# A two-layer graph network on one core: deeper buffer rings and longer lags in the message stages

## The reference, cut to what matters

```
h = relu(layernorm(x));  x = x + layer0(h, edge_attr_16, edge_attr_4, src, dst)
h = relu(layernorm(x));  x = x + layer1(h, edge_attr_3, edge_attr_64, src, dst)

layer0, for each edge:  w = silu(edge_scalars @ Wfc1) @ Wfc2            (192 weights)
    e = (h @ Wl1)[src];  mid = products of w, e and edge_attr_4
    n = mean of mid over the edges with the same dst;  out = sc + alpha(n) * (n @ Wl2)
layer1, for each edge:  w = relu(edge_feature @ W_fc1) @ W_fc2          (224 weights)
    xs, xv = (h @ W_nl)[dst];  tp = products of w, xs, xv and the unit vector of edge_attr_3
    agg = sum of tp over the edges with the same src / 32;  out = gated(agg @ W_out + h @ W_skip)
```

## Time and profile before

| | |
|---|---|
| median of 3 runs | 12,249.92 us (12,239.58 to 12,279.39) |
| the profiled execution | 12,298.2 us, its span 12,296.4 us |
| messages, layer 0 | about 2,794 to 7,952 us |
| messages, layer 1 | about 8,718 to 12,010 us |
| busy shares of the span | PE 60%, DVE 61%, POOL 59%, ACT 41% |
| DMA engines | 20% for the software queue (POOL), 17.5% for SP's |

### The profile page before, as it was taken

How to read it: one execution, slowest core, us unless ns; L and a number is a source line. 1 busy time by engine, 2 the same in 40 slices (tenths; PEclk the granted TensorE clock), 3 DMA queues, 4 the chain that set the end, 5 groups by cost and what they waited for, 6 DMA issues and landing times. The chain is left out here.

```text
span 12296.4 us, 187070 instructions
## 1 busy us (share of the span) xinstructions
PE 7410.2 (60%) x31320; PEld 4866.9 (40%) x31320; DVE 7443.2 (61%) x21099; ACT 4992.3 (41%) x16585; POOL 7196.8 (59%) x7101
## 2 busy tenths in 40 slices
PE   4444444445555555555555555577667777777777
PEld 3222222222222222222222222255566666666667
DVE  6444444445565565555555565576667777777763
ACT  2333333333333333333333333343445555555553
POOL 4666666656666666666666666555555666665650
PEclk7555555557777777777777777788899999999999
DMA  2222222223333333333333334444444444444465
GB/s 80 74 74 74 73 73 72 74 69 108 106 109 107 109 110 108 108 109 107 107 108 109 109 108 108 92 148 143 120 116 127 128 122 124 128 128 122 129 114 166
DMA packets 854401, 1321.82 MB, mean 107 GB/s; under 512 B 253376, under 2 KB 655040, under 8 KB 854208
## 3 DMA queue, kind: packets, MB, share of 16 engines
q0 software_dynamic: 339456, 670.10, 20.0%
q1 hardware_dynamic: 469232, 606.08, 17.5%
q10 hardware_dynamic: 45648, 44.94, 1.3%
HBM read 868.56 MB, written 918.54 MB: 145 GB/s over the span
## 5 line engine op out<-in xcount | busy, mean ns | idle before, releaser
L1396 POOL DMA_INDIRECT feat_m<-feat_tab,rows_m x3744 | 3867.9, 1033 | 2929.9 <-DMA rows_m<-sorted_rows 1401.3
L1470 PE MATMUL bank<-prod_m,hot_m 128*128 128x449 f32 x3744 | 2329.6, 761 | 2211.0 <-issue 646.9
L1493 PE MATMUL pair<-prod_m,hot_m 128*128 128x160 f32 x14976 | 2386.6, 316 | 930.1 <-DVE prod_m L1679 621.6
L1493 PEld LDWEIGHTS pair<-prod_m,hot_m 128*128 128x128 f32 x14976 | 2203.1, 201 | 1114.1 <-issue 1114.0
L1526 ACT ACTIVATE prod_m<-part_m,rows_m 128x64 f32<-128x64 f32 x5616 | 1442.4, 337 | 2812.9 <-DVE part_m L1665 1890.2
L1514 ACT ACTIVATE hot_m<-hot_m,rows_m 128x128 f32<-128x128 f32 x5616 | 1742.7, 388 | 1565.9 <-DVE hot_m L1648 1194.7
L600 POOL DMA_INDIRECT sorted_rows<-rows_e,place_e x1664 | 1634.9, 983 | 1051.8 <-issue 520.7
L1470 PEld LDWEIGHTS bank<-prod_m,hot_m 128*128 128x128 f32 x3744 | 858.1, 252 | 3446.1 <-issue 3285.3
L1413 POOL DMA_INDIRECT sorted_rows<-later_m,place_m x1248 | 1274.2, 1021 | 380.9 <-issue 369.9
L1711 DVE SCALAR_TENSOR_TENSOR acc_m<-acc_m,same_block,bank 128x449 f32<-128x449 f32 x936 | 636.5, 680 | 1294.6 <-remote 731.3
L1679 DVE TENSOR_TENSOR prod_m<-rows_m,feat_m 128x192 f32<-128x192 f32 (+1 forms) x4680 | 1226.9, 311 | 0.0
(11 more groups left out here) (241 smaller groups left out, 8767.3 us busy)
## 6 DMA issues: line engine op xcount, KB each, us to landing
agg_tab<-acc_m SPq DMA_DIRECT2D x936, 320.0 KB
rows_m<-sorted_rows SPq DMA_DIRECT2D x936, 229.0 KB
agg_tab<-acc_m SPq DMA_DIRECT2D x936, 224.5 KB
rows_m<-sorted_rows SPq DMA_DIRECT2D x936, 197.0 KB
feat_m<-feat_tab,rows_m POOLq DMA_INDIRECT x3744
turned_m<-in_turned ACTq DMA_DIRECT2D x159, 256.0 KB
agg_s<-agg_tab SPq DMA_DIRECT2D x98, 320.0 KB, 2.7
sorted_rows<-rows_e,place_e POOLq DMA_INDIRECT x1664
```

Of the source, the lines that this page charges most:

```text
L1396: pool.indirect_dma_start(out=feat[s % RING][:, k, :], out_offset=None, in_=g.feat_tab[l.n], in_offset=bass.IndirectOffsetOnAxis(ap=rows[s ...
L1470: mm = pe.matmul(out[:, 0, :], hot[s % HOTS][:, k, 0, :], prod[s % prods][:, k, 0:l.agg], start=(k == 0), stop=(k == ST_TILES - 1))
L1493: mm = pe.matmul(dst, hot[s % HOTS][:, k, q, :], rhs, start=(k == 0 and col == 0), stop=(k == ST_TILES - 1), skip_group_check=True)
```

## The change

All constants below belong to `messages`. The row ring grows from 6 to 12 buffers; feature buffers stay at 6 under a name of their own (FRING). One-hots, products, parts, accumulators and PSUM result banks are 4 each (before 3, 2 or 3, 2, 3 and 2). The running sum is made five steps behind in place of three, its store issued ten behind in place of five. The work on layer 1's rows is spread over six steps in place of four, and its scatters have a table of their own (SENDS); PSUM is cut into four pairs of banks. The release order of semaphores at the end of `sort_edges` is changed as well.

```diff
-RING = 6
-HOTS = 3
-STORE_LAG = 5
+RING = 12
+FRING = 6
+HOTS = 4
+STORE_LAG = 10
+ADD_LAG = 5
-WINDOW = {s: (j, i) for j, s0 in enumerate((0, 6)) for i, s in enumerate(range(s0, s0 + 4))}
+WINDOW = {s: (j, i) for j, s0 in enumerate((0, 6)) for i, s in enumerate(range(s0, s0 + 6))}
+SENDS = {9: (0, 0), 10: (0, 1), 11: (0, 2), 0: (-2, 3), 3: (-1, 0), 4: (-1, 1), 5: (-1, 2), 6: (-1, 3)}
+SEND_TAIL = 7
...
-        g.ps = [est.enter_context(nc.psum_tensor(f"bank{i}", [P, 512], F32)) for i in range(2)]
-        g.ps2 = [est.enter_context(nc.psum_tensor(f"pair{i}", [P, 2, 512], F32)) for i in range(3)]
+        g.ps2 = [est.enter_context(nc.psum_tensor(f"pair{i}", [P, 2, 512], F32)) for i in range(4)]
+        g.ps = [g.ps2[3][:, n, :] for n in range(2)]
...
-            w_bank = [g.ps2[0][:, 0, :], g.ps2[0][:, 1, :], g.ps2[1][:, 0, :], g.ps2[1][:, 1, :]]
-            res = [g.ps[s][:, 0:l.agg].rearrange("p (o c) -> p o c", o=1) for s in range(2)]
+            w_bank = {0: g.ps2[0][:, 0, :], 2: g.ps2[0][:, 1, :], 1: g.ps2[0][:, 0, :], 3: g.ps2[0][:, 1, :]}
+            res = [b[:, 0:l.agg].rearrange("p (o c) -> p o c", o=1) for b in (g.ps[0], g.ps[1], g.ps2[1][:, 0, :], g.ps2[1][:, 1, :])]
...
             def gather(step, it, s):
                 u = it * TURN + s
                 pool.wait_ge(rows_here[s % RING], 16 * (use(it, s, RING) + 1))
-                if step is None or step >= RING:
-                    pool.wait_ge(prod_ready, u - RING + 1)
+                if step is None or step >= FRING:
+                    pool.wait_ge(prod_ready, u - FRING + 1)
...
             def send(step, it, s):
-                if s not in WINDOW:
+                if s not in SENDS:
                     return
-                j, i = WINDOW[s]
-                h, c = (j - 1) % 2, it * PER_TURN + j - 1
+                back, i = SENDS[s]
+                h, c = back % 2, it * PER_TURN + back
+                if step is not None and not 0 <= c < NCHUNK0:
+                    return
...
-                if step is None or step >= 2:
-                    pe.wait_ge(acc_ready, u)
+                if step is None or step >= HOTS:
+                    pe.wait_ge(acc_ready, u - HOTS + 2)
...
-                stage(3, add_up)(step, it, s)
-            turns(dve, NST, TURN, step_, tail=3)
+                stage(ADD_LAG, add_up)(step, it, s)
+            turns(dve, NST, TURN, step_, tail=ADD_LAG)
```

More of the change, by code:

```diff
@@ L897, in sort_edges @@
     nc.gpsimd.sem_clear(range(first, last + 1))
-    for u in used:
+    by_transfers = {u.num for u in (s_zero, s_const, s_in, s_fc, s_w, s_wz, s_neg, *turned_here, *meta_here, *s_key,
+                                    *rows_sent, *stored)}
+    for u in sorted(used, key=lambda v: v.num in by_transfers):
         nc.release_semaphore(u)
@@ L1315, in messages @@
         if sends:
-            part = [sb(f"part{s}", [P, ST_TILES, S0 + V0], F32) for s in range(2)]
+            part = [sb(f"part{s}", [P, ST_TILES, S0 + V0], F32) for s in range(HOTS)]
             part_ready, inner_ready, outer_ready = (sem(x) for x in ("part_ready", "inner_ready", "outer_ready"))
@@ L1419, in step_ @@
                     gather(step, it, s)
-                if sends and (step is None or step >= 4):
+                if sends:
                     send(step, it, s)
-            turns(pool, NST, TURN, step_, tail=4 if sends else 0)
+            turns(pool, NST, TURN, step_, tail=SEND_TAIL if sends else 0)
             if sends:
@@ L1447, in prepare @@
                     hidden(1 - h, n + h)
-                for part in (1, 2):
+                for odd, part in enumerate((1, 4)):
                     w = window(step, it, s, part)
@@ L1461, in sums @@
                 u = it * TURN + s
-                out = res[s % 2]
+                out = res[s % HOTS]
                 pe.wait_ge(hot_ready, u + 1)
@@ L1520, in outer @@
                 act.wait_ge(part_ready, u * 2 + 1)
[L1521 to L1522 removed]
+                if step is None or step >= HOTS:
+                    act.wait_ge(sum_ready, u - HOTS + 1)
                 for k in range(ST_TILES):
@@ L1542, in load_meta, with evict @@
                               ).then_inc(meta_here[h], 16)
+            def evict(c, h, odd):
+                for i in PAIRS[2 * odd:2 * odd + 2]:
+                    act.wait_ge(w_ready, c * 4 + 2 * odd + 2)
+                    act.activation(later[h][:, 2 * i:2 * i + 2, 0:L1.wnum].bitcast(F32),
+                                   w_bank[i][:, 0:2 * L1.wnum].rearrange("p (k c) -> p k c", k=2), ACT.Copy
+                                   ).then_inc(evicted, 1)
             def prepare(step, it, s):
-                w = window(step, it, s, 0)
+                w = window(step, it, s, 2)
                 if w is not None:
                     c, h, n, known = w
+                    act.wait_ge(norm, c * 2 + 2)
+                    if known >= 1:
+                        act.wait_ge(inverse, c)
+                    act.activation(dist[1][:, :], dist[0][:, :], ACT.Sqrt).then_inc(root_ready, 1)
                     if known >= 1:
@@ L1553, in prepare @@
                     c, h, n, known = w
+                    if known >= 2:
+                        act.wait_ge(sent[h], CHUNK_TILES * 16 * n)
+                    evict(c, h, 0)
+                w = window(step, it, s, 5)
+                if w is not None:
+                    c, h, n, known = w
+                    act.wait_ge(r.ranked, c * 2 + 2)
+                    act.activation(place[h][:, :], r.rank_f[h][:, :], ACT.Copy).then_inc(r.place_here, 1)
+                    evict(c, h, 1)
                     act.wait_ge(copied, c + 1)
                     load_meta(c + 2, h)
-                for part in (1, 2):
-                    w = window(step, it, s, part)
-                    if w is not None:
-                        c, h, n, known = w
-                        if part == 1:
-                            act.wait_ge(norm, c * 2 + 2)
-                            if known >= 1:
-                                act.wait_ge(inverse, c)
-                            act.activation(dist[1][:, :], dist[0][:, :], ACT.Sqrt).then_inc(root_ready, 1)
-                            if known >= 2:
-                                act.wait_ge(sent[h], CHUNK_TILES * 16 * n)
-                        for i in PAIRS[2 * part - 2:2 * part]:
-                            act.wait_ge(w_ready, c * 4 + 2 * part)
-                            act.activation(later[h][:, 2 * i:2 * i + 2, 0:L1.wnum].bitcast(F32),
-                                           w_bank[i][:, 0:2 * L1.wnum].rearrange("p (k c) -> p k c", k=2), ACT.Copy
-                                           ).then_inc(evicted, 1)
-                        if part == 2:
-                            act.wait_ge(r.ranked, c * 2 + 2)
-                            act.activation(place[h][:, :], r.rank_f[h][:, :], ACT.Copy).then_inc(r.place_here, 1)
             def step_(step, it, s):
@@ L1595, in _ @@
             if sends:
-                for s in range(prods):
+                for s in range(HOTS):
                     dve.memset(prod[s][:, :, l.ones_at:l.ones_at + 1], 1.0)
@@ L1617, in prepare @@
                     dve.tensor_reduce(dist[0][:, :], sq[:, :, :], AX.X, ALU.add).then_inc(norm, 1)
-                w = window(step, it, s, 1)
+                w = window(step, it, s, 2)
                 if w is not None:
@@ L1624, in prepare @@
                     bin_hot(nc, dve, r, g, c + 1, 1 - h, c if known >= 1 else None)
-                w = window(step, it, s, 2)
+                w = window(step, it, s, 4)
                 if w is not None:
@@ L1710, in add_up @@
                 half = lambda a: a[:, :].rearrange("p (h c) -> p h c", h=n)
-                dve.scalar_tensor_tensor(half(acc[q]), half(prev), same, res[s % 2], ALU.mult, ALU.add).then_inc(acc_ready, 1)
+                dve.scalar_tensor_tensor(half(acc[q]), half(prev), same, res[s % HOTS], ALU.mult, ALU.add).then_inc(acc_ready, 1)
             def step_(step, it, s):
```

45 lines of the change are left out of this document (21 added, 24 removed).

## The result

The changed kernel takes 12,342.01 us (12,314.11 to 12,371.41, nine runs) against 12,275.77 us (12,239.58 to 12,292.02, nine runs) for the one before: ratio 1.0058, 95% interval 1.0046 to 1.0071. The profiled execution took 12,358.05 us, its span 12,355.9. The forecast was 12,351 us.

A forecast was written before the change was run, and what follows sets the result against it. SP's instruction stream, slowed while POOL issues without a break, was taken to bound both message stages. Terms -26 + 117 + 10 = +101 us on a median of 12,250 gave 12,351 us, range 12,150 to 12,520 us.

The forecast's parts named there:

- SP bounds both stages and has no waits to lose: Both message stages: SP runs its program without pause yet late; its queue waits only 52.2 us in all.
- the first rival: Message stages: late rows are the limit and twelve buffers cure it, 1,810 us faster, 10,440 us; chance 7%.
- -26 us for SP's waits: SP's queue, both stages: deeper row ring and later store remove waits, gain 0 to 52 us, half taken.
- +117 us for register instructions: SP's loop, both stages: 912 more register instructions at 0.128 us each; bounds 30 to 257 us.
- the third rival: SP's loop: the extra instructions cost next to nothing, total 12,238 to 12,287 us; chance 24%.
- +10 us at the stages' ends: SP's last stores in both stages: the last sum comes two DVE steps later, twice, +10 us.
- Nothing for the sum's new wait "while SP leads": DVE's `add_up` needs the store of SP's step u+6; other engines have some steps of slack, priced at nothing.
- My last rival: DVE tied to SP's stores falls behind until POOL lacks features: 882 us at most, by half 12,790 us; chance 5%.
- Nothing for the four buffers, the sum's lag of five and the spread of layer 1's features: PE, DVE, ACT and POOL in the message stages: these edits lie beside SP's pace, priced at nothing.
- the second rival: Layer 0: DVE holds POOL up, its runs break, SP's slow spells become fewer; 256 us less, 12,095 us; chance 9%.
- What would show it: Signs expected in the changed profile: smaller SP waits, POOL's row wait over 900 us, both stages 1 to 2% longer.
- the 5.4 that I had named as a sign of being wrong: Layer 0: a mean SP step under 5.4 us would show the prediction wrong.

The follow-up runs named there:

- ring-12 kernel: The kernel before with 12 row buffers in place of 6, its lags and other buffers kept: 12,562.54 us, ratio 0.9996.
- lot C: Experiments run together on one chip, where the kernel before took 12,495 us; the changed kernel run again there had ratio 1.0040.
- lot B: Experiments run together on another chip, where the kernel before, run again unchanged, took 12,518 us, ratio 0.9996.
- A: Lot of experiments run together on a chip of its own, where the kernel before took 12,568 us.
- light SP: Bounds assertions of SP's table read left out, six of 16 instructions: on the kernel before 12,426.16 us (0.9868), on the changed kernel 12,181.31 us (0.9737).

## Why the prediction was right in size and wrong in its terms

*SP bounds both stages and has no waits to lose: held in the main.* SP's waits were 52.2 us and are 16.6; the ring alone gives 0.9996, and the first rival (the ring cures the rows) is out. But it held for one reason less than I thought. I argued that SP's own program length is the bound. A step with 1.59 instructions more cost 0.4%; one with six fewer gave 1.3%, but there the wait for the sum took over, so that run doesn't price them. SP is bound by its slow spells beside POOL. That the program's length mainly sets how SP shares the time with them is my reading of the split above, not a thing shown by itself.

*-26 us for SP's waits: not to be measured.* They fell by 36 us in the changed kernel, which is less than a difference of 0.3% (37 us). The ring-12 kernel doesn't price the term, since its waits didn't fall.

*+117 us for register instructions: the mis-sized term.* 0.128 us each was taken, 0.018 was measured, so 912 of them make 16 us; in the ring-12 kernel, which has them and little else, nothing shows (0.9970 to 1.0022). The row I sized it by, an undisturbed step, is the wrong place: with 2,888 more instructions the slow spells shrank by 137 us where the rest grew by 130 (layer 0), and by 99 where it grew by 142 (layer 1). I had that reason in the text and used it to pick a point between the bounds; it was the third rival, and for this term the rival was right. The attribution was wrong too (ring, not lag).

*+10 us at the stages' ends.* From the last row load to the last store layer 0 takes 42.7 us in place of 19.4, layer 1 21.1 in place of 17.9: +27 us.

*Nothing for the sum's new wait "while SP leads": the step that failed.* SP doesn't lead. It was shown to be late everywhere else in the prediction, and a wait of DVE on SP's step u+6 hangs on just that late engine. It is 2,145 us of DVE's waiting, of which some 630 us are more idle time than before. My last rival had the mechanism, but asked for POOL to run out of feature buffers. In layer 1, where the time was lost, POOL waits for them less than before (116.5 us, before 190.2); in layer 0 it waits more (224.6, before 11.3), and that stage got shorter. The way that the wait costs is another one. A stretch of layer 1 in the changed kernel, POOL, then DVE's `add_up`, then SP:

```profile
9606.78 0.87 DVE L1719 SCALAR_TENSOR_TENSOR acc_m<-acc_m,same_block,pair 128x640 f32<-128x640 f32 x1
9607.57 0.48 DVE L1656 SCALAR_TENSOR_TENSOR hot_m<-iota_n,base_node,rows_m 128x256 f32<-128x256 f32 x1
9607.97 0.49 DVE L1680 TENSOR_TENSOR prod_m<-rows_m,feat_m 128x128 f32<-128x128 f32 x2
9608.37 0.96 DVE L1687 TENSOR_TENSOR prod_m<-rows_m,feat_m 128x192 f32<-128x192 f32 x4
9612.57 0.88 DVE L1719 SCALAR_TENSOR_TENSOR acc_m<-acc_m,same_block,pair 128x640 f32<-128x640 f32 x1 [3.24 <-DMA agg_tab<-acc_m]
...
9607.38 0.95 POOL L1401 DMA_INDIRECT feat_m<-feat_tab,rows_m  x1 [0.30 <-issue]
9608.63 1.52 POOL L1401 DMA_INDIRECT feat_m<-feat_tab,rows_m  x1 [0.30 <-issue]
9614.93 1.01 POOL L1401 DMA_INDIRECT feat_m<-feat_tab,rows_m  x1 [4.79 <-DMA rows_m<-sorted_rows]
...
9603.97 0.33 SPq L1380 DMA_DIRECT2D rows_m<-sorted_rows  x1
9606.77 0.71 SPq L1387 DMA_DIRECT2D agg_tab<-acc_m  x1
9611.55 0.34 SPq L1380 DMA_DIRECT2D rows_m<-sorted_rows  x1
9612.28 0.10 SPq L1387 DMA_DIRECT2D agg_tab<-acc_m  x1
```

POOL issues a run of gathers; SP is slow through it (7.58 us from row load to row load); its store goes out at 9612.28 and DVE, which stood 3.24 us, goes on within 0.3 us; POOL has run dry meanwhile. The gather of 9608.63 runs beside L1687 and takes 1.52 us. In the changed kernel (lot C) a gather that overlaps an instruction of L1687 takes 1,248 ns in layer 1 and one that doesn't 950; before (lot B) it was 1,078 beside the same product and 961 without. POOL's mean unbroken run in layer 1 grows from 3.0 to 5.1 us (lots B and C), and SP's slow time with it, by the 161 us that the stage lost. With the store eight behind the wait goes, the run falls to 2.5 us, and the loss with it. That the wait causes layer 1's loss is shown by that run, in which one constant differs. How a halted DVE makes POOL's runs longer, step for step, I read from timelines only; it isn't shown.

The Trainium skill, page "SBUF — State Buffer", section "Who interferes with whom", says that a vector instruction with two inputs in SBUF contends with a GpSimd instruction that reads SBUF. The trace agrees for L1687, whose two inputs lie in SBUF (1,248 beside 950 ns); it adds that the same overlap costs 1,045 against 969 ns with the store eight behind, where POOL's runs are short, so the overlap alone doesn't set the price.

*Nothing for the four buffers, the sum's lag of five and the spread of layer 1's features: wrong by some 110 to 130 us of gain in layer 0.* Layer 0 is 111 us shorter in the changed kernel (C against B), 131 with the ring of 6, 125 with the store eight behind (A), and 1 us without these edits (ring-12 kernel). So the gain needs neither the ring nor DVE's wait for the store. It isn't the second rival as I put it, shorter runs of POOL: they got longer, 14.6 us against 10.6. Which of the three edits gives it wasn't tried, and stays open. With the store eight behind, layer 1 too is 68 us shorter than in the ring-12 twin, about as much as single stages differ without a cause known.

*What would show it.* Eight register operations a turn and the smaller waits of SP came. POOL's wait for rows "over 900 us in layer 0" didn't (560), nor "both stages longer by 1 to 2%" (-1.9% and +4.7%), and SP's step in layer 0 is 5.36 us from row load to row load (5.40 as the prediction took it, the stage over 936), at the edge of the 5.4 that I had named as a sign of being wrong. By these signs the mechanism was wrong in part. That the forecast was close is luck: the total came out at +66 us (12,342 less 12,276, the median of before over nine runs) beside +101 because a gain of 100 and a loss of 155 us, neither in the sum, partly cancel.

## What to carry to other kernels

A deeper ring gave nothing where the producer had no slack (0.9996): look first at whether its queue waits at all. If it doesn't, lightening the producer in the same change can make ring and lags pay (here 1.004 alone, and with the light SP from 0.9868 to 0.9737). When a lag is lengthened, write down for each wait which step of the other engine it now needs; a wait on the late engine's future step turned 0.984 into 1.004, though the producer was the same. And a step's price can't be read from its undisturbed copy where two engines slow each other: test the coupling itself by breaking it up.

## What of the hardware was not expected

- SP's instructions are mostly slow, many of 0.70 us, where POOL has issued indirect DMAs back to back for over 5 us (76% of them over 0.55 us apart in layer 0 before, 10% where POOL issues nothing), and work put between them makes the program faster: 16 memsets of 544 ns a turn, ratio 0.9663. What is shared between the two isn't known from these runs.
- 2,888 more instructions on the engine that bounds cost 0.018 us each.
- An indirect DMA's issue is 0.95 us long by itself, and has a second common length of 2.16 us beside DVE's work. Over 1.9 us take 46 (before), 194 (changed) and 508 (changed, light SP) of 1,872 in layer 1.
- PE's granted clock in layer 1 differs between these kernels: a mean of 0.95 of full speed before, 0.89 in the changed kernel, 0.97 with the store eight behind, so mostly the upper of its two levels (2.4 GHz) with stretches at the lower (1.2 GHz). PE's busy time rose from 2,387 to 2,526 us in the changed kernel. It doesn't carry the loss: `add_up` waits 17.5 us for PE there, before 343.9.
